# Turning each tile's rows one step later in a mixture-of-experts feed-forward: before this tile's gate and up products instead of after the tile's two places ahead

## The chip, the cores and the metric

The kernel runs on one core of one Trainium2 chip. The metric is the device time of one execution in microseconds (us); smaller is better. The kernel before takes 4045.59 us, the median of 3 runs (4045.33 to 4053.72).

## The reference, cut to what matters

The input is 8192 rows of 512 numbers. A modulated linear layer gives `xf`; a feed-forward follows that adds a shared expert and 8 of 64 routed experts for each row; the input is added at the end. Routing biases make the experts' sizes very unequal.

```python
# y: modulated 512x512 layer with a clip; xf = y.reshape(8192, 512)
shared = silu(xf @ sh_gate_w) * (xf @ sh_up_w) @ sh_down_w            # hidden 1024
topk_idx, w = _route(xf, router_w, e_bias)                            # 8 of 64 experts
order = argsort(topk_idx.reshape(-1), stable=True); tok = order // K
g = ragged_dot(xf[tok], gate_w, group_sizes)                          # 512 -> 256
u = ragged_dot(xf[tok], up_w, group_sizes)
o = ragged_dot(silu(g) * u, down_w, group_sizes)                      # 256 -> 512
routed = zeros_like(xf).at[tok].add(o * w.reshape(-1)[order][:, None])
return x + (shared + routed)
```

## The kernel before

The program has a dense phase (the modulated layer, the shared expert, the routing; some 1430 us) and a routed phase, which the change touches. In the routed phase the rows of each expert stand in tiles of 128 rows: 532 tiles, handled in one loop in groups of four (`UN = 4`; tile j has place `u = j % 4`). Each engine has its own in-order program, written by hand, and they meet at semaphores.

What happens to a tile j:
- SyncE loads two index lists; GpSimd gathers the 128 rows of `y_rows` into `x_rows` by an indirect DMA (L1036).
- TensorE turns the rows in four 128x128 transposes (`turn_x`, L1090). ScalarE copies them from PSUM as the high part `x_h` in fp32r (`x_high`, L1161), VectorE takes the rest, `x_l` (`x_low`, L30).
- TensorE does gate and up together: 4 slices of the contraction, for each the products high*high, high*low, low*high, 12 matmuls of 512 columns (`gate_up`, L1099). It waits for `x_l` of the tile and for `split`, which counts the parts of the expert's weights that VectorE has finished.
- ScalarE `silu` (L1167) and VectorE `hidden` (L1258) make `e_hf`; TensorE turns it (`turn_h`, 2 transposes in fp32, L1108); ScalarE and VectorE part it in `e_h_h` (L1173) and `e_h_l` (L30).
- TensorE `down` (L1117): 6 matmuls of 512 columns; ScalarE `weigh` (L1181) scales the result to `o_rows`; GpSimd adds it to the output by an indirect DMA (L1052).

One step of TensorE works on three tiles: gate and up of j, the turned rows of j+2, `turn_h` of j-1, `down` of j-2. A new expert's weights (three DMAs of 512 KB issued by SyncE, L998 and L1000) are cast on ScalarE (L1186) and parted on VectorE (L30, `w_gu_l`, `w_dn_l`); this happens in 29 places, two steps ahead of the expert's first tile: part 0 (`w_gu`, 1536 columns) in one step, parts 1 and 2 (512 and 1024 columns) at the beginning of VectorE's next step.

Of the kernel before, what the change touches and what calls it, by code (L numbers as in the profile page):

```python
# [32 lines left out]
def build(nc, x, cond, cw, cbias, aff_w, aff_b, router_w, e_bias, gate_w, up_w, down_w,  # L33
# [18 lines left out]
    UN = 4  # L52
# [17 lines left out]
    with top:  # L70
# [46 lines left out]
        with ExitStack() as tmp:  # L117
# [29 lines left out]
            @blk.sync  # L147
            def _(sp):
                sp.dma_start(aw_raw[:], aff_w.rearrange("(k p) w -> p k w", p=P)).then_inc(ld_aff, 16)
                sp.dma_start(cond_raw[:], cond).then_inc(ld_aff, 16)  # L150
                sp.dma_start(w_raw[:], cw.rearrange("(k p) c -> p k c", p=P)).then_inc(ld_w, 16)
                sp.dma_start(rw_raw[:], router_w).then_inc(ld_r, 16)
                with nc.allow_non_contiguous_dma(reason="small columns"):
                    sp.dma_start(ab[:], aff_b.rearrange("(k p) -> p k", p=P)).then_inc(ld_small, 16)
                    sp.dma_start(bias_c[:], cbias.rearrange("(k p) -> p k", p=P)).then_inc(ld_small, 16)
                sp.dma_start(eb[:], e_bias.partition_broadcast(P)).then_inc(ld_small, 16)
                for n, w in enumerate((sh_gate, sh_up, sh_down)):
                    if n == 1:
                        sp.dma_start(xin[:], xf[0:TB, :].rearrange("(t p) c -> p t c", p=P)).then_inc(x_ld, 16)
                    sp.dma_start(stage[n][:], w.rearrange("(k p) h -> p k h", p=P)).then_inc(ld_sh[n], 16)  # L160
# [740 lines left out]
        with ExitStack() as tmp:  # L901
# [42 lines left out]
            def field(eng, j, f, top_val):  # L944

                return eng.value_load(trow[0:1, bass.ds(j * FLD + f, 1)], min_val=0 if f != 5 else 4, max_val=top_val)  # L946
# [134 lines left out]
            @blk.tensor  # L1081
            def _(pe):
                pe.wait_ge(tab_ld, 16)
                pe.sem_inc(pe_do, 1)

                def turn_x(j, u, g):

                    pe.wait_ge(x_ld[u], 16 * (g + 1))
                    for k in range(KC):
                        last = nc.tensor.transpose(b_x[u % 2][:, k * P:(k + 1) * P].bitcast(F32R),  # L1090
                                                   xg[u][:, k * P:(k + 1) * P].bitcast(F32R), ident_r[:])
                    last.then_inc(pe_x, 1)

                def gate_up(j, u, place):

                    pe.wait_ge(dve_x, j + 1)
                    for k in range(KC):
                        for a, b in ((0, 0), (0, 1), (1, 0)):
                            last = nc.tensor.matmul(b_gu[u % 2][:], xp[a][:, u % 2, k, :],  # L1099
                                                    wgu[b][:, bass.ds(place, 1), k, :].rearrange("p a n -> p (a n)"),  # L1100
                                                    start=(k == 0 and a == b == 0), stop=(k == KC - 1 and a == 1))
                    last.then_inc(pe_gu, 1)

                def turn_h(j, u):

                    pe.wait_ge(dve_gu, j + 1)
                    for k in range(KH):
                        last = nc.tensor.transpose(b_h[u % 2][:, k * P:(k + 1) * P], hf[:, u % 2, k * P:(k + 1) * P], ident[:])  # L1108
                    last.then_inc(pe_ht, 1)

                def down(j, u, place):
                    if not isinstance(j, int) or j >= 2:
                        pe.wait_ge(act_do, j - 1)
                    pe.wait_ge(dve_ht, j + 1)
                    for k in range(KH):
                        for a, b in ((0, 0), (0, 1), (1, 0)):
                            last = nc.tensor.matmul(b_o[u % 2][:], hp[a][:, u % 2, k, :],  # L1117
                                                    wdn[b][:, bass.ds(place, 1), k, :].rearrange("p a n -> p (a n)"),
                                                    start=(k == 0 and a == b == 0), stop=(k == KH - 1 and a == 1))
                    last.then_inc(pe_do, 1)  # L1120

                def step(g, u, turn):

                    j = g * UN + u
                    place = turn.place(u)
                    pe.wait_ge(split, 3 * turn.order(u) + 3 + SPLIT_0)
                    gate_up(j, u, place)
                    turn_x(j + 2, (u + 2) % UN, g + 1 if u >= UN - 2 else g)
                    if not isinstance(j, int) or j >= 1:
                        turn_h(j - 1, (u - 1) % UN)  # L1130
                    if not isinstance(j, int) or j >= 2:
                        down(j - 2, (u - 2) % UN, turn.place(u - 2))

                pe.wait_ge(ident_ok, 1)
                pe.wait_ge(words, 1)
                turn_x(0, 0, 0)
                turn_x(1, 1, 0)
                for g in range(2):
                    turn = Turn(pe, g)
                    for u in range(UN):  # L1140
                        step(g, u, turn)
                last_turn = field(pe, 0, 5, NTURN - 1)
                with pe.Fori(2, NTURN) as g:
                    with pe.If(last_turn >= g):
                        turn = Turn(pe, g)
                        for u in range(UN):
                            step(g, u, turn)
                end = UN * last_turn + UN - 1
                turn_h(end, UN - 1)
                down(UN * last_turn + UN - 2, UN - 2, field(pe, UN * last_turn + UN - 2, 1, E) & (RING - 1))  # L1150
                down(end, UN - 1, field(pe, end, 1, E) & (RING - 1))

            @blk.scalar
            def _(act):
                act.wait_ge(tab_ld, 16)

                def x_high(j, u):
                    act.wait_ge(pe_x, j + 1)
                    if not isinstance(j, int) or j >= 2:
                        act.wait_ge(pe_gu, j - 1)  # L1160
                    nc.scalar.copy(xp[0][:, u % 2, :, :].rearrange("p k t -> p (k t)"), b_x[u % 2][:]).then_inc(act_x, 1)  # L1161
# [13 lines left out]
                def weigh(j, u, g):  # L1175

                    act.wait_ge(pe_do, j + 2)
                    act.wait_ge(ls_ld[u], 16 * (g + 1))
                    if not isinstance(j, int) or j >= UN:
                        act.wait_ge(added[u], 16 * g)  # L1180
                    nc.scalar.activation(og[u][:], b_o[u % 2][:], ACT.Copy, scale=ls[u][:, 1:2].bitcast(F32)).then_inc(act_do, 1)  # L1181
# [21 lines left out]
                def step(g, u, turn):  # L1203
                    j = g * UN + u
                    known = isinstance(j, int)
                    if not known or j >= 3:
                        weigh(j - 3, (u - 3) % UN, g - 1 if u < 3 else g)
                    with act.If(turn.first(u + 2) > 0):
                        start_weights(j + 2, turn.order(u + 2))
                    silu(j, u)  # L1210
                    x_high(j + 2, (u + 2) % UN)
                    if not known or j >= 1:
                        h_high(j - 1, (u - 1) % UN)
                    with act.If(turn.first(u + 2) > 0):
                        end_weights(turn.order(u + 2))
# [2 lines left out]
                start_weights(None, 0)  # L1218
                end_weights(0)
                x_high(0, 0)  # L1220
                x_high(1, 1)
                turn = Turn(act, 0)
                with act.If(turn.first(1) > 0):
                    start_weights(None, turn.order(1))
# [19 lines left out]
            def _(dve):  # L1244
# [4 lines left out]
                def x_low(j, u):  # L1249
                    dve.wait_ge(act_x, j + 1)  # L1250
                    sub_exact(nc, xp[1][:, u % 2, :, :].rearrange("p k t -> p (k t)"), b_x[u % 2][:],
                              xp[0][:, u % 2, :, :].rearrange("p k t -> p (k t)")).then_inc(dve_x, 1)
# [22 lines left out]

                def step(g, u, turn):
                    j = g * UN + u
                    with dve.If(turn.first(u + 1) > 0):
                        weights_low(turn.order(u + 1), (1, 2))
                    hidden(j, u)  # L1280
                    x_low(j + 2, (u + 2) % UN)
                    if not isinstance(j, int) or j >= 1:
                        h_low(j - 1, (u - 1) % UN)
                    with dve.If(turn.first(u + 2) > 0):
                        weights_low(turn.order(u + 2), (0,))
# [23 lines left out]
                dve.wait_ge(words, 1)  # L1309
                weights_low(0, (0, 1, 2))  # L1310
                x_low(0, 0)
                x_low(1, 1)
                turn = Turn(dve, 0)
                with dve.If(turn.first(1) > 0):
                    weights_low(turn.order(1), (0,))
# [40 lines left out]
```

## Time and profile before

| | us |
|---|---|
| median of 3 runs | 4045.59 |
| the profiled execution's own time | 4045.33 |
| its span, first to last instruction | 4043.6 |
| PE busy | 3891.3 (96%) |
| PEld busy | 3190.3 (79%) |
| POOL, DVE, ACT busy | 1916.6, 1649.8, 1444.2 |

PE is TensorE's matmuls, PEld its loads of the stationary operand, which can run beside a matmul. A matmul's shown duration contains its way through the array, so neighbouring ones overlap in the rows; what one costs is the distance from its start to the next start. DVE is VectorE, ACT ScalarE, POOL GpSimd, SP SyncE. Two consecutive instructions of one kind stand in one row of the timeline, with their count.

### The profile page before, as it was taken

How to read it: one execution, taken by the hardware profiler on the slowest of the kernel's cores; microseconds unless marked ns; L12 is line 12 of the kernel's file. 1: busy time of each engine (PE TensorE's matmuls, PEld its weight loads, DVE VectorE, ACT ScalarE, POOL GpSimd, SP SyncE). 2: the span in 40 equal slices, each digit the busy share in tenths (PEclk: the TensorE clock that was granted, in tenths of full speed). 3: DMA queues.
4: the chain of work that ended last, by engine and by line, in shares of the span. 5: the costliest groups of instructions: out<-in, count | busy, mean ns of one | idle time of the engine just before them, and what ended most of it. 6: DMA issues, size and time to landing. Idle time of an engine off the chain costs nothing.

```text
span 4043.6 us, 90661 instructions
## 1 busy us (share of the span) xinstructions
PE 3891.3 (96%) x19158; PEld 3190.3 (79%) x19159; DVE 1649.8 (41%) x3503; ACT 1444.2 (36%) x2807; POOL 1916.6 (47%) x1598
## 2 busy tenths in 40 slices
PE   7999999999999879999999999998899999999997
PEld 6888788888888658888888877886688888888886
DVE  4555555555555433333332333334433333333332
ACT  3222222222222123433433444445434343444333
POOL 1333333333333535555555555554455555555554
PEclk9999999999999889999999999999999999999998
DMA  5112211122111056666766666777776666676665
GB/s 175 42 48 58 64 43 43 48 58 63 42 42 50 24 107 114 124 116 112 138 115 114 126 133 125 125 128 194 168 119 123 116 125 114 126 127 125 114 113 104
DMA packets 372970, 408.94 MB, mean 101 GB/s; under 512 B 192457, under 2 KB 227409, under 8 KB 372881
## 3 DMA queue, kind: packets, MB, share of 16 engines
q0 software_dynamic: 135872, 280.60, 38.6%
q1 hardware_dynamic: 237010, 127.35, 12.4%
q8 instruction: 34, 0.56, 0.1%
q14 instruction: 54, 0.44, 0.1%
HBM read 228.83 MB, written 178.93 MB: 101 GB/s over the span
## 4 chain that ended last, share of the span: by engine, by line
PE 41%; DMA 9%; SPq 6%; issue 6%; DVE 0%; ACT 0%; POOLq 0%; DVEq 0%; ACTq 0%; POOL 0%
PE bank L1099 24%; PE bank L1117 12%; DMA out_dram<-o_rows,list_s 6%; SPq L946 4%; PE bank L1090 3%; PE bank L1108 2%; DMA list_g<-slot_list 2%; SPq L981 2%; DMA raw_d<-in_L_ffn_down_w_dram 1%; DMA raw_gu<-in_L_ffn_up_w_dram 1%; SPq L998 0%; DVE w_dn_l L30 0%; POOLq L946 0%; DMA list_s<-slot_list 0%; SPq L1000 0%
## 5 line engine op out<-in xcount | busy, mean ns | idle before, releaser
L1052 POOL DMA_INDIRECT out_dram<-o_rows,list_s x532 | 862.0, 1620 | 668.4 <-issue 352.5
L1258 DVE TENSOR_TENSOR e_hf<-bank,e_sg 128x256 f32<-128x256 f32 x532 | 225.8, 424 | 1669.0 <-ACT e_sg L1167 965.5
L406 POOL DMA_INDIRECT slot_list<-ent,pos x512 | 498.6, 974 | 860.6 <-PE bank L430 708.1
L1099 PE MATMUL bank<-w_gu_h,x_h 128*128 x2128 | 842.2, 396 | 33.9 <-DVE w_dn_l L30 31.3
L1099 PE MATMUL bank<-w_gu_h,x_l 128*128 x2128 | 837.5, 394 | 0.0
L1099 PE MATMUL bank<-w_gu_l,x_h 128*128 x2128 | 832.9, 391 | 0.0
L1036 POOL DMA_INDIRECT x_rows<-y_rows,list_g x536 | 536.9, 1002 | 563.0 <-issue 345.9
L1167 ACT ACTIVATE e_sg<-bank 128x256 f32<-128x256 f32 x532 | 204.6, 385 | 985.5 <-PE bank L1099 687.3
L1181 ACT ACTIVATE o_rows<-bank,list_s 128x512 f32<-128x512 f32 x532 | 367.0, 690 | 444.8 <-PE bank L1117 390.4
L1099 PEld LDWEIGHTS bank<-w_gu_h,x_h 128*128 128x128 f32 x2128 | 402.1, 189 | 130.8 <-issue 47.6
L1117 PE MATMUL bank<-w_dn_h,e_h_h 128*128 x1064 | 472.1, 444 | 4.8 <-DVE e_h_l L30 2.5
L1099 PEld LDWEIGHTS bank<-w_gu_h,x_l 128*128 128x128 f32 x2128 | 402.3, 189 | 91.1
L1099 PEld LDWEIGHTS bank<-w_gu_l,x_h 128*128 128x128 f32 x2128 | 402.4, 189 | 87.4
L1117 PE MATMUL bank<-w_dn_h,e_h_l 128*128 x1064 | 422.4, 397 | 0.0
L1117 PE MATMUL bank<-w_dn_l,e_h_h 128*128 x1064 | 419.8, 395 | 0.0
L30 DVE TENSOR_TENSOR x_l<-bank,x_h 128x512 fp32r<-128x512 f32 x534 | 369.1, 691 | 31.0 <-ACT x_h L1161 3.1
L1090 PEld LDWEIGHTS bank<-ident_r,x_rows 128*128 128x128 f32 x2136 | 240.0, 140 | 109.2 <-issue 25.7
L1161 ACT CAST x_h<-bank 128x512 fp32r<-128x512 f32 x534 | 313.5, 587 | 6.0 <-PE bank L1090 5.8
L1090 PE MATMUL bank<-ident_r,x_rows 128*128 128x128 f32 x2136 | 246.4, 239 | 35.8 <-DMA x_rows<-y_rows,list_g 35.6
L1117 PEld LDWEIGHTS bank<-w_dn_h,e_h_l 128*128 128x128 f32 x1064 | 200.8, 189 | 52.5
L616 ACT CAST h_h<-stage_d 128x512 fp32r<-128x512 f32 x128 | 79.4, 620 | 425.1 <-DVE stage_d L688 362.9
L1117 PEld LDWEIGHTS bank<-w_dn_h,e_h_h 128*128 128x128 f32 x1064 | 201.5, 189 | 33.9 <-issue 7.4
(203 smaller groups left out, 5711.2 us busy)
## 6 DMA issues: line engine op xcount, KB each, us to landing
xin<-in_x_dram SPq DMA_DIRECT2D x16, 1024.0 KB
y_rows<-yrow SPq DMA_DIRECT2D x64, 256.0 KB
stage_d<-in_x_dram SPq DMA_DIRECT2D x16, 1024.0 KB
out_dram<-stage_d SPq DMA_DIRECT2D x16, 1024.0 KB
raw_gu<-in_L_ffn_gate_w_dram SPq DMA_DIRECT2D x29, 512.0 KB
raw_gu<-in_L_ffn_up_w_dram SPq DMA_DIRECT2D x29, 512.0 KB
raw_d<-in_L_ffn_down_w_dram SPq DMA_DIRECT2D x29, 512.0 KB
list_g<-slot_list SPq DMA_DIRECT2D x536, 1.0 KB
```

Of the source, the lines that this page charges most:

```text
L30: return nc.vector.tensor_tensor(out, full, high.bitcast(F32), ALU.subtract)
L406: nc.gpsimd.indirect_dma_start(slots, bass.IndirectOffsetOnAxis(ap=pos[v][:, t, k:k + 1], axis=0), ent[v][:, t, k, :], None).then_inc(scat ...
L946: return eng.value_load(trow[0:1, bass.ds(j * FLD + f, 1)], min_val=0 if f != 5 else 4, max_val=top_val)
L1036: nc.gpsimd.indirect_dma_start(xg[u][:], None, y_rows, bass.IndirectOffsetOnAxis(ap=lg[u][:, 0:1].bitcast(U32), axis=0)).then_inc(x_ld[u], 16)
L1052: nc.gpsimd.indirect_dma_start(out, bass.IndirectOffsetOnAxis(ap=ls[u][:, 0:1].bitcast(U32), axis=0), og[u][:], None, compute_op=ALU.add). ...
L1090: last = nc.tensor.transpose(b_x[u % 2][:, k * P:(k + 1) * P].bitcast(F32R), xg[u][:, k * P:(k + 1) * P].bitcast(F32R), ident_r[:])
L1099: last = nc.tensor.matmul(b_gu[u % 2][:], xp[a][:, u % 2, k, :], wgu[b][:, bass.ds(place, 1), k, :].rearrange("p a n -> p (a n)"), start=( ...
L1117: last = nc.tensor.matmul(b_o[u % 2][:], hp[a][:, u % 2, k, :], wdn[b][:, bass.ds(place, 1), k, :].rearrange("p a n -> p (a n)"), start=(k ...
L1161: nc.scalar.copy(xp[0][:, u % 2, :, :].rearrange("p k t -> p (k t)"), b_x[u % 2][:]).then_inc(act_x, 1)
L1167: nc.scalar.activation(sg[:, u % 2, :], b_gu[u % 2][:, 0:H], ACT.Silu).then_inc(act_gu, 1)
L1181: nc.scalar.activation(og[u][:], b_o[u % 2][:], ACT.Copy, scale=ls[u][:, 1:2].bitcast(F32)).then_inc(act_do, 1)
L1258: nc.vector.tensor_tensor(hf[:, u % 2, :], b_gu[u % 2][:, H:2 * H], sg[:, u % 2, :], ALU.mult).then_inc(dve_gu, 1)
```

## The change

`turn_x`, `x_high` and `x_low` work one tile ahead, at the beginning of a step, and no longer two tiles ahead in its middle. TensorE's step becomes: turn j+1, gate and up of j, `turn_h` of j-1, `down` of j-2. On ScalarE `x_high` stands ahead of `weigh` and of the weights' first cast; it stood behind `silu`. On VectorE `x_low` stands ahead of the weights' parts 1 and 2; it stood behind `hidden`. The second tile's turn ahead of the loop goes.

```diff
@@ TensorE
 def step(g, u, turn):
     j = g * UN + u
+    turn_x(j + 1, (u + 1) % UN, g + 1 if u == UN - 1 else g)
     place = turn.place(u)
     pe.wait_ge(split, 3 * turn.order(u) + 3 + SPLIT_0)
     gate_up(j, u, place)
-    turn_x(j + 2, (u + 2) % UN, g + 1 if u >= UN - 2 else g)
     if not isinstance(j, int) or j >= 1:
         turn_h(j - 1, (u - 1) % UN)
...
 turn_x(0, 0, 0)
-turn_x(1, 1, 0)
@@ ScalarE
+    x_high(j + 1, (u + 1) % UN)
     if not known or j >= 3:
         weigh(j - 3, (u - 3) % UN, g - 1 if u < 3 else g)
     with act.If(turn.first(u + 2) > 0):
         start_weights(j + 2, turn.order(u + 2))
     silu(j, u)
-    x_high(j + 2, (u + 2) % UN)
...
 x_high(0, 0)
-x_high(1, 1)
@@ VectorE
+    x_low(j + 1, (u + 1) % UN)
     with dve.If(turn.first(u + 1) > 0):
         weights_low(turn.order(u + 1), (1, 2))
     hidden(j, u)
-    x_low(j + 2, (u + 2) % UN)
...
 x_low(0, 0)
-x_low(1, 1)
```

TensorE in a step of the loop, before: the last of the 12 gate and up matmuls, then both kinds of transposes in a row.

```order
L1099 MATMUL bank<-w_gu_h,x_l 128x512
L1088 ISA
L1090 MATMUL bank<-ident_r,x_rows 128x128 [waits x_rows_ld2]
L1090 MATMUL bank<-ident_r,x_rows 128x128 x3
L1108 MATMUL bank<-ident,e_hf 128x128 [waits dve_gu]
L1108 MATMUL bank<-ident,e_hf 128x128
```

The same place now:

```order
L1099 MATMUL bank<-w_gu_h,x_l 128x512
L1108 MATMUL bank<-ident,e_hf 128x128 [waits dve_gu]
L1108 MATMUL bank<-ident,e_hf 128x128
L1113 REGISTER_ALU
L1114 REGISTER_ALU [waits act_do]
```

And the passage from `down` to the next gate and up, now:

```order
L1117 MATMUL bank<-w_dn_h,e_h_l 128x512
L1090 MATMUL bank<-ident_r,x_rows 128x128 [waits x_rows_ld2]
L1090 MATMUL bank<-ident_r,x_rows 128x128 x3
L1127 REGISTER_ALU x2
L1127 ISA
L1096 REGISTER_ALU [waits split]
L1099 REGISTER_ALU [waits dve_x]
L1099 ISA
L1099 MATMUL bank<-w_gu_h,x_h 128x512
```

The six short matmuls between two long ones have become four ahead of gate and up, and two ahead of `down`.

VectorE where a new expert's weights are parted, before (`x_l` stands after the weights and `e_hf`):

```order
L30 TENSOR_TENSOR w_gu_l<-raw_gu,w_gu_h 128x1536
L1284 UNCONDITIONAL_BRANCH
L1278 COMPARE_AND_BRANCH
L1268 ISA
L30 REGISTER_ALU [waits w_high]
L30 ISA
L30 REGISTER_ALU
L30 ISA
L30 TENSOR_TENSOR w_gu_l<-raw_gu,w_gu_h 128x512
```

The same place now:

```order
L30 TENSOR_TENSOR w_gu_l<-raw_gu,w_gu_h 128x1536
L1282 UNCONDITIONAL_BRANCH
L30 TENSOR_TENSOR x_l<-bank,x_h 128x512 [waits act_x]
L1277 COMPARE_AND_BRANCH
L1266 ISA
L30 REGISTER_ALU [waits w_high]
L30 ISA
L30 REGISTER_ALU
L30 ISA
L30 TENSOR_TENSOR w_gu_l<-raw_gu,w_gu_h 128x512
```

`x_l`, with its wait for ScalarE's `act_x`, now stands between the first part of the weights and the other two.

## Rows read from the trace of the kernel before

**Rows 1.** The page: the chain that ended last, shares of the span

```profile
PE 41%; DMA 9%; SPq 6%; issue 6%; DVE 0%; ACT 0%; POOLq 0%; DVEq 0%; ACTq 0%; POOL 0%
```

**Rows 2.** Timeline of one step, matmuls: start us, us, engine, line, operation, count

```profile
3000.20 0.40 PE L1099 MATMUL bank<-w_gu_h,x_h 128*128 x1
...
3002.94 0.46 PE L1090 MATMUL bank<-ident_r,x_rows 128*128 128x128 f32 x4
3003.23 0.41 PE L1108 MATMUL bank<-ident,e_hf 128*128 128x128 f32 x2
...
3004.88 0.40 PE L1099 MATMUL bank<-w_gu_h,x_h 128*128 x1
...
3009.57 0.40 PE L1099 MATMUL bank<-w_gu_h,x_h 128*128 x1
```

**Rows 3.** Timeline of the same step, loads from the fp32 transposes on

```profile
3003.20 0.20 PEld L1108 LDWEIGHTS bank<-ident,e_hf 128*128 128x128 f32 x2
...
3003.26 0.14 PEld L1108 LDWEIGHTS bank<-ident,e_hf 128*128 128x128 f32 x1
3003.37 0.19 PEld L1117 LDWEIGHTS bank<-w_dn_h,e_h_h 128*128 128x128 f32 x1
3003.48 0.19 PEld L1117 LDWEIGHTS bank<-w_dn_l,e_h_h 128*128 128x128 f32 x1
3003.72 0.19 PEld L1117 LDWEIGHTS bank<-w_dn_h,e_h_l 128*128 128x128 f32 x1
```

**Rows 4.** Timeline of the dense phase, loads after 64-column bf16 matmuls

```profile
97.45 0.19 PEld L497 LDWEIGHTS bank<-mask,ones 128*128 128x128 bf16 x4
97.57 0.19 PEld L430 LDWEIGHTS bank<-sh_down_h,h_h 128*128 128x128 f32 x1
97.68 0.19 PEld L430 LDWEIGHTS bank<-sh_down_l,h_h 128*128 128x128 f32 x1
```

**Rows 5.** Timeline of the dense phase, loads after eight transposes

```profile
137.88 0.19 PEld L430 LDWEIGHTS bank<-cols_l,sh_gate_h 128*128 128x128 f32 x1
...
140.42 0.19 PEld L430 LDWEIGHTS bank<-cols_h,sh_up_h 128*128 128x128 f32 x1
...
141.10 0.19 PEld L430 LDWEIGHTS bank<-cols_h,sh_up_h 128*128 128x128 f32 x1
```

**Rows 6.** Timeline of the step of rows 2, VectorE and ScalarE

```profile
3004.05 0.69 DVE L30 TENSOR_TENSOR x_l<-bank,x_h 128x512 fp32r<-128x512 f32 x1
3005.08 0.69 ACT L1181 ACTIVATE o_rows<-bank,list_s 128x512 f32<-128x512 f32 x1 [0.79 <-issue]
```

**Rows 7.** Waits, routed phase: engine, line, what for, us in total, times, longest

```profile
PE bank L1099 <- DVE w_dn_l L30: 31.3, 24, 2.1
...
PEld bank L1090 <- DMA x_rows<-y_rows,list_g: 13.5, 10, 3.3
...
SPq L946 <- DMA out_dram<-o_rows,list_s: 280.2, 207, 7.4
```

**Rows 8.** Timeline at a new expert's weights, ScalarE, VectorE and PE

```profile
3691.45 1.48 ACT L1186 CAST w_gu_h<-raw_gu  x1 [1.92 <-DMA raw_gu<-in_L_ffn_up_w_dram]
...
3694.33 0.41 DVE L30 TENSOR_TENSOR e_h_l<-bank,e_h_h 128x256 fp32r<-128x256 f32 x1
...
3694.36 1.06 ACT L1186 CAST w_dn_h<-raw_d  x1
...
3694.96 1.76 DVE L30 TENSOR_TENSOR w_gu_l<-raw_gu,w_gu_h  x1 [0.22 <-issue]
3697.03 0.69 DVE L30 TENSOR_TENSOR w_gu_l<-raw_gu,w_gu_h  x1 [0.30 <-issue]
3697.63 1.22 DVE L30 TENSOR_TENSOR w_dn_l<-raw_d,w_dn_h  x1
...
3699.19 0.51 PE L1099 MATMUL bank<-w_gu_h,x_h 128*128 x1 [1.14 <-DVE w_dn_l L30]
```

**Rows 9.** Waits from 2764 to 2920 us, where small experts follow each other

```profile
PEld bank L1090 <- DMA x_rows<-y_rows,list_g: 13.1, 9, 3.3
```

## The prediction

> **What bounds the kernel now.** I read the page's chain first: TensorE has 41% of it and no other engine's work shows at all [rows 1]; the waits and DMAs that share it are ones that TensorE mostly does not stand still for. Then the timeline of one step far from a weight change. Gate and up of one tile start at 3000.20, of the next at 3004.88, of the next at 3009.57: a step takes 4.69 us, with TensorE never idle [rows 2]. 532 steps of 4.69 are 2495 us of the routed phase, so what happens inside TensorE's own stream is the term to get right. Last the waits: TensorE stands still for the weights' last part (31.3 us in 24 places) and for gathered rows (13.5 us, 10 places) [rows 7]. All other engines have slack in a plain step.
>
> **TensorE's step, by starts.** Nothing is added or taken from a step: 18 long matmuls (512 columns), 4 transposes of `x_rows`, 2 of `e_hf`. Only neighbours change, so I price the borders. [...] Behind a long matmul (0.23 from start to start) every load is hidden. Behind a short one it may not be. The rows give the borders:
> - The loads of `e_hf` begin at 3003.20 and 3003.26 [rows 3]: 0.06 apart. So behind the last `x_rows` transpose, the first `e_hf` load costs no more than 0.06.
> - The next load begins at 3003.37 (0.11 for the fp32 transpose), the one after at 3003.48: again 0.11, either the second transpose or the load of `e_h_h` [rows 3].
> - Which of the two it is tells the dense phase: behind bf16 matmuls that follow each other by 0.03 (four loads in 0.19), the fp32r operand's load begins at 97.57 and the next at 97.68 [rows 4]. With nothing long ahead of it an fp32r load costs 0.11 by itself.
>
> Before, the six short ones stand together: four `x_rows`, two `e_hf`, then `down`. After, `x_h`'s first load stands behind the last `x_rows` transpose: 0.11 instead of the 0.06 of `e_hf`. The first `e_hf` load is now behind a long matmul and hidden; its transpose (0.11) and `down`'s first load (0.11) are as before. The border of `down` to gate and up (0.23) becomes `down` to `x_rows` (0.23), that of gate and up to `x_rows` becomes gate and up to `e_hf` (0.23). Net: 0.11 - 0.06 = 0.05 us a step; times 532, **27 us slower**.
>
> [...]
>
> **A second, smaller term.** Long matmuls are a little slower for a while after short ones. In the dense phase, the 11 loads from 137.88 to 140.42 follow eight transposes and take 2.54, 0.231 each; the next three take 0.68, 0.227 each [rows 5]. So one burst costs 0.04 over the next ten or so. The routed step pays this once now: the 12 from 3000.20 to 3002.94 take 2.74, only 0.02 over 12 times 0.227 [rows 2], since they are the tail's end; the rest of the tail lies in `down`. With two bursts, gate and up pay their own tail, 0.04 instead of 0.02. `down` pays as before, or less because only two short ones stand ahead of it. From both sides: +0.03 a step if both tails are whole, -0.04 if they shrink with the burst; the dense rows are the nearest for gate and up, so I take +0.015, **8 us** in 532 steps.
>
> **What the late turn costs the other engines.** Counted from the first `x_rows` transpose (3002.94) to the end of `x_l` (3004.05 + 0.69) it takes 1.8 us [rows 2, 6]. Now the turn of j+1 starts about 0.3 ahead of gate and up of j, and the result is wanted a step later, after 4.7. Some 2.9 us of slack stay: no cost in a plain step. If something held `x_high` for longer than that, TensorE would wait for the difference. `weigh` has to stand behind `x_high`: `o_rows` begins 0.2 after the first gate and up matmul now [rows 2, 6]; it will begin about 0.7 after it. Its PSUM bank is not wanted for more than a step, so the 0.5 costs nothing there, but the scatter, and behind it SyncE, which waits for scatters 207 times [rows 7], start 0.5 us later relative to TensorE. Behind SyncE's wait stand the index lists and the weights' DMAs. The lists feed gathers whose turn is 1.9 us later than before, so they gain; the weights lose up to 0.5 us.
>
> **At a new expert.** The chain runs from the cast of `w_gu_h` at 3691.45, once the DMA has landed, to gate and up at 3699.19: 7.7 us [rows 8]. VectorE does in it `e_hf`, `x_l`, `e_h_l` and then the three parts of the weights. After, the same work stands in another order: `e_hf`, `e_h_l`, part 0 (0.7 us earlier), `x_l`, parts 1 and 2. The new head of the queue, `x_l`, waits for ScalarE's `x_high`, which stands behind the two last weight casts, and for TensorE to have turned j+2 after `down`. ScalarE's last cast ends 4.0 after 3691.45 now (3694.36 + 1.06); with `x_high` (about 0.6, an estimate from `x_l`'s 0.69 on the same elements) taken from ahead of it that is 3.4 or 3.5, and `x_high` ends at 4.1. Part 0 ends 5.3 after now (3694.96 + 1.76), 4.6 then [rows 8]. So `x_l` just fits and the 7.7 stays. I cost the 24 waits at 0.1 us each for their later landing (0.5 later, less what five longer steps of lead, 0.07 each, give back): **3 us**. From both sides: -0.7 each if VectorE's earlier start shortened the chain, +0.7 each if `x_l` waits, so -17 to +17.
>
> **Gathered rows.** 13.5 us in 10 places [rows 7], of which 13.1 in 9 places lie where small experts follow each other [rows 9] and the weights end the wait anyway. I count nothing; at most 10 us go. One turn, one `x_high`, one `x_low` go at the end: -0.4.
>
> **Sum.** 27 + 8 + 3 - 0.4 = 38 us against the profiled execution's own 4045.33 (span 4043.6, 1.7 around it), which is the median of the runs to 0.3: **4083 us**, 0.9% slower.
>
> **The rivals.**
> - [...] Chance 0.08.
> - *A faster kernel.* The place is VectorE's queue at a new expert. If part 0, 0.7 us earlier, brings the last part 0.7 earlier in 24 waits, that is 17 us; with the gather waits gone, another 10. That is 27 us, and together with a border that costs nothing and a tail that does not grow, 4045 - 27 = 4018. It wins once the border costs under 0.05 us a step. For it: `x_l` stands later now, and rows wait longer to be turned. Against it: parts 1 and 2 still stand behind `x_l`. Chance 0.04.
> - *A new wait on x.* `x_high` or TensorE's order makes `x_l` late at each new expert, and gate and up of plain steps wait at times. If the 29 changes of weights cost 0.7 each, that is 20 us on top of 35: 4101. For it: the fit above is half a microsecond. Chance 0.13.
> - Forecast, the borders and tails: chance 0.75.
>
> **Range and chances.** The likeliest case alone reaches from 27 - 9 to 27 + 17 + 5, that is 4063 to 4094, and the new wait to 4101. I give 4062 to 4097. What a measurement of this kernel tells from no change is 0.2%, 8 us. Slower by more: 0.75 + 0.13, and a third of the first rival: 0.91. Faster by more: 0.04. Within: 0.05.
>
> **What would show it.** In the profile after, a plain step from one gate and up to the next takes 4.75 (right: 4.73 to 4.77; 4.69 says that the border is hidden). The second load of gate and up begins 0.11 after the first, and 0.23 between the two `e_hf` loads. The waits for `w_dn_l` stay near 31 us; over 50 says that `x_l` is in the way. Waits for gathered rows go down. I am wrong if the step is the same, or if the time comes from another wait than TensorE's stream.

## The result, and the profile after

| | before | after |
|---|---|---|
| median of 4 runs | 4049.65 us (4045.33 to 4055.8) | 4081.88 us (4079.21 to 4090.57) |
| ratio | | 1.0082, 95% interval 1.0059 to 1.0105 |
| span of the profiled execution | 4043.6 us | 4088.2 us |

The kernel is slower by 0.8%. The forecast was 4083 us. That the time itself came out within 1 us of it is in part luck: the forecast was 38 us more than 4045.33, the medians measured here are 32.2 us apart (24 to 43 by the interval), and the kernel before was 4 us slower in this comparison. The profiled execution after is one of the slower ones: its span is 44.6 us longer, of which 7.3 lie ahead of the routed phase, in the dense phase that the change does not touch. The granted clock of TensorE was 0.78 there in the first 101 us, and 0.97 in the profile before; at 111 us the profile after is already 4.3 us behind. The first turn of rows starts at 1442.58 before and at 1449.88 after. These two rows are of before and then of after, matmuls by start:

```profile
1442.58 0.72 PE L1090 MATMUL bank<-ident_r,x_rows 128*128 128x128 f32 x4 [24.92 <-DMA x_rows<-y_rows,list_g]
```

```profile
1449.88 0.72 PE L1090 MATMUL bank<-ident_r,x_rows 128*128 128x128 f32 x4 [24.53 <-DMA x_rows<-y_rows,list_g]
```

From the first gate and up to the last it is 2563.5 us before and 2602.1 after, 38.6 more. That is the change's.

A plain step after, matmuls (start, duration, both in us), answers to [rows 2]:

```profile
3002.46 0.46 PE L1090 MATMUL bank<-ident_r,x_rows 128*128 128x128 f32 x4
3002.76 0.46 PE L1099 MATMUL bank<-w_gu_h,x_h 128*128 x1
...
3005.60 0.38 PE L1108 MATMUL bank<-ident,e_hf 128*128 128x128 f32 x2
...
3007.22 0.46 PE L1090 MATMUL bank<-ident_r,x_rows 128*128 128x128 f32 x4
3007.51 0.46 PE L1099 MATMUL bank<-w_gu_h,x_h 128*128 x1
```

From one turn of rows to the next it is 4.76 us, 0.07 more than the 4.69 before. Over all plain steps the median is 4.687 before and 4.760 after, and it hardly varies. 531 intervals of 0.073 are 38.8 us: the whole difference of the routed phase.

The loads of the same step (PEld), which answer to [rows 3], show where the 0.07 is:

```profile
3002.72 0.19 PEld L1099 LDWEIGHTS bank<-w_gu_h,x_h 128*128 128x128 f32 x1
3002.83 0.19 PEld L1099 LDWEIGHTS bank<-w_gu_l,x_h 128*128 128x128 f32 x1
3003.06 0.19 PEld L1099 LDWEIGHTS bank<-w_gu_h,x_l 128*128 128x128 f32 x1
...
3005.37 0.37 PEld L1108 LDWEIGHTS bank<-ident,e_hf 128*128 128x128 f32 x2
...
3005.60 0.14 PEld L1108 LDWEIGHTS bank<-ident,e_hf 128*128 128x128 f32 x1
3005.71 0.19 PEld L1117 LDWEIGHTS bank<-w_dn_h,e_h_h 128*128 128x128 f32 x1
3005.82 0.19 PEld L1117 LDWEIGHTS bank<-w_dn_l,e_h_h 128*128 128x128 f32 x1
```

From the load of `x_h` behind the last turned row to the next load it is 0.11 (3002.72 to 3002.83), where it was 0.06 from the load of `e_hf`. The first `e_hf` load now lies under a long matmul: 0.23 to the second. From there it is 0.11 and 0.11 to the next two, as before. The 11 loads from 3002.83 to 3005.37 take 2.54, just what the 11 loads behind eight transposes of the dense phase took [rows 5].

TensorE's waits of the routed phase after answer to [rows 7]:

```profile
PE bank L1099 <- DVE w_dn_l L30: 40.0, 27, 3.2
PE bank L1090 <- DMA x_rows<-y_rows,list_g: 25.8, 2, 24.5
PE bank L1108 <- DVE e_hf L1256: 13.0, 6, 5.6
```

The second row is now only the start of the phase (24.5 us, which the window of rows 7 left out). Waits for gathered rows in the loop are gone. Waits for the weights went from 31.3 to 40.0 us, and 13.0 us for `e_hf` are there. The 531 intervals from one gate and up to the next, less 531 plain steps, hold 74.7 us before and 74.5 after: outside plain steps nothing was gained or lost, as far as one profile each can tell.

Waits are not all that these 75 us hold. TensorE's waits of the loop, all rows of the answer without the one at the end of the phase, are 50.1 us before and 55.5 after. Some of the rest is the granted clock. In these rows of the kernel before, the clock is at the upper of its two levels at first (granted clock 1.00) and at the lower one (0.50 from 2797.7 to 2801.1) soon after a wait:

```profile
2796.28 0.49 PE L1099 MATMUL bank<-w_gu_h,x_h 128*128 x1 [2.10 <-DVE w_dn_l L30]
2796.61 0.39 PE L1099 MATMUL bank<-w_gu_l,x_h 128*128 x1
2796.84 0.39 PE L1099 MATMUL bank<-w_gu_h,x_l 128*128 x1
...
2798.24 0.63 PE L1099 MATMUL bank<-w_gu_l,x_h 128*128 x1
2798.66 0.63 PE L1099 MATMUL bank<-w_gu_h,x_l 128*128 x1
```

A long matmul then takes 0.43 us from start to start instead of 0.23. Every such fall within the loop, in this trace and in that of the kernel after, comes behind a wait of 1.4 us or more. At the lower level the loop spends 34 us before, some 30 of them with TensorE at work, and 27 us after. By 0.43 against 0.23 that costs some 14 us before and 11 after, an estimate. The forecast had no term for it.

### The profile page after: what moved, and what is told of

The parts are those of the page before. It is cut to its first block, busy times and chain, and to the rows that moved or that the text cites. A ratio compares the mean times of both kernels' runs of the same rounds, so it can differ in the third digit from the quotient of the medians.

```text
span 4088.2 us, 90388 instructions
## 1 busy us (share of the span) xinstructions
PE 3924.2 (96%) x19154; PEld 3196.6 (78%) x19155; DVE 1649.8 (40%) x3502; ACT 1435.3 (35%) x2806; POOL 1937.9 (47%) x1598
## 4 chain that ended last, share of the span: by engine, by line
PE 48%; DMA 7%; SPq 4%; issue 4%; DVE 0%; POOLq 0%; DVEq 0%; ACT 0%; POOL 0%; ACTq 0%
PE bank L1099 29%; PE bank L1117 14%; DMA out_dram<-o_rows,list_s 4%; PE bank L1090 3%; SPq L946 2%; PE bank L1108 2%; DMA raw_d<-in_L_ffn_down_w_dram 1%; DMA list_g<-slot_list 1%; SPq L981 1%; SPq L998 0%; DVE w_dn_l L30 0%; POOLq L946 0%; DMA raw_gu<-in_L_ffn_up_w_dram 0%; SPq L1000 0%; POOL x_rows L1036 0%
## 5 line engine op out<-in xcount | busy, mean ns | idle before, releaser
L1052 POOL DMA_INDIRECT out_dram<-o_rows,list_s x532 | 871.9, 1639 | 804.4 <-DMA list_g<-slot_list 455.3
L1099 PE MATMUL bank<-w_gu_h,x_h 128*128 x2128 | 883.4, 415 | 40.3 <-DVE w_dn_l L30 40.0
L1036 POOL DMA_INDIRECT x_rows<-y_rows,list_g x536 | 545.9, 1018 | 446.7 <-issue 277.6
L30 DVE TENSOR_TENSOR e_h_l<-bank,e_h_h 128x256 fp32r<-128x256 f32 x532 | 220.8, 415 | 7.1 <-ACT e_h_h L1172 7.1
```

The lines of the kernel that those rows point to most:

```text
L30: return nc.vector.tensor_tensor(out, full, high.bitcast(F32), ALU.subtract)
L1036: nc.gpsimd.indirect_dma_start(xg[u][:], None, y_rows, bass.IndirectOffsetOnAxis(ap=lg[u][:, 0:1].bitcast(U32), axis=0)).then_inc(x_ld[u], 16)
L1052: nc.gpsimd.indirect_dma_start(out, bass.IndirectOffsetOnAxis(ap=ls[u][:, 0:1].bitcast(U32), axis=0), og[u][:], None, compute_op=ALU.add). ...
```

## The experiments

Each was timed beside the kernel before on the same chip. That kernel's median differs from chip to chip (4020.94 us beside the first four, 4046.62 beside the next four, 4041.58 beside the last), so only ratios to it are compared. Waits and clocks are of one profile of each kernel.

### TensorE's order alone

```diff
-                    gate_up(j, u, place)
-                    turn_x(j + 2, (u + 2) % UN, g + 1 if u >= UN - 2 else g)
+                    pe.wait_ge(dve_x, j + 1)
+                    turn_x(j + 2, (u + 2) % UN, g + 1 if u >= UN - 2 else g)
+                    gate_up(j, u, place)
```

> The kernel before, still turning rows two tiles ahead, with ScalarE's and VectorE's programs untouched; on TensorE alone the turn of j+2 is put ahead of gate and up of j (behind the wait for x_l of j, which frees its PSUM bank). Theory A (the price is in TensorE's stream: a load behind the last short transpose costs 0.11 instead of 0.06 us, and a second burst makes the following long matmuls a little slower): a plain step takes 4.76 us as in the kernel after, the whole about 38 us more than before, ratio 1.008 to 1.010. Rival B (the price is the later turn of the rows, or the new places of x_high and x_low on ScalarE and VectorE): a plain step stays at 4.69, ratio 1.000.

Measured: ratio 1.009 (1.0075 to 1.0104). From turn to turn:

```profile
3000.97 0.46 PE L1090 MATMUL bank<-ident_r,x_rows 128*128 128x128 f32 x4
...
3005.73 0.46 PE L1090 MATMUL bank<-ident_r,x_rows 128*128 128x128 f32 x4
```

4.76 us, and the same loss as the whole change, with the rows turned two tiles ahead and the other engines' programs untouched. The price is TensorE's order. Rival B, that it is the later turn or the new places on ScalarE and VectorE, falls.

The order also moved the waits. These rows answer to [rows 7]:

```profile
PE bank L1090 <- DMA x_rows<-y_rows,list_g: 40.1, 20, 3.6
...
PE bank L1090 <- DVE w_dn_l L30: 4.0, 6, 2.0
```

The turn now stands first in TensorE's step, so TensorE waits there for late rows (40.1 us, 9.2 before) and hardly for the weights any more (4.0, 31.3 before).

### The change with one burst

```diff
                     turn_x(j + 1, (u + 1) % UN, g + 1 if u == UN - 1 else g)
+                    if not isinstance(j, int) or j >= 1:
+                        turn_h(j - 1, (u - 1) % UN)
                     place = turn.place(u)
...
                     gate_up(j, u, place)
-                    if not isinstance(j, int) or j >= 1:
-                        turn_h(j - 1, (u - 1) % UN)
```

> The kernel after, with the two transposes of e_hf put right behind the four of x_rows, ahead of gate and up: six short matmuls in one burst again, the rows still turned only one tile ahead. Theory A: the borders are those of before (0.06 for the first e_hf load, 0.11 for the fp32r load behind an fp32 transpose), a plain step 4.69, the whole within 10 us of before, ratio 0.998 to 1.002. Rival B (the later turn costs): 4.76 and 1.009 stay.

Measured: ratio 1.0023 (1.0014 to 1.0032). A plain step, and TensorE's largest wait:

```profile
3000.13 0.46 PE L1090 MATMUL bank<-ident_r,x_rows 128*128 128x128 f32 x4
3000.42 0.41 PE L1108 MATMUL bank<-ident,e_hf 128*128 128x128 f32 x2
3000.59 0.49 PE L1099 MATMUL bank<-w_gu_h,x_h 128*128 x1
...
3004.82 0.46 PE L1090 MATMUL bank<-ident_r,x_rows 128*128 128x128 f32 x4
```

```profile
PE bank L1108 <- DVE e_hf L1256: 44.2, 20, 8.6
```

The plain step is back at 4.69, so the loss goes with the burst and not with the later turn: this is theory A's main sentence. The whole, 11.5 us by the medians, is just outside what I gave. The `e_hf` transposes now stand ahead of gate and up, and at new experts TensorE waits 44.2 us for them in 20 places. But these waits took the place of others: all of TensorE's waits in the loop are 48.6 us, 50.1 in the kernel before. Over plain steps the intervals hold 85 us all the same, where those of the kernel before hold 75 and those of the first experiment's kernel 63. What did grow is the time at the lower clock level, 51 us of the loop instead of 34 (granted clock 0.94 from 2600 to 3000, and 0.96 before): by the prices above some 6 of the 10 us, an estimate. No run changes the clock by itself, so this is read from the traces and not shown.

### The two e_hf transposes first

```diff
-                    turn_x(j + 2, (u + 2) % UN, g + 1 if u >= UN - 2 else g)
                     if not isinstance(j, int) or j >= 1:
                         turn_h(j - 1, (u - 1) % UN)
+                    turn_x(j + 2, (u + 2) % UN, g + 1 if u >= UN - 2 else g)
```

> The kernel before, with the two e_hf transposes ahead of the four of x_rows: one burst of six as before, in the other order. Theory A by the loads: after the hidden first load 0.11, 0.11, 0.08, 0.08, 0.09 and then 0.11 for down's fp32r load behind a short transpose, 0.59 instead of 0.54: a plain step 4.73 to 4.75, about 27 us more than before, ratio 1.0065. Rival C (each separate burst of short matmuls costs 0.07, whatever is loaded): still one burst, so 4.69 and ratio 1.000.

Measured: ratio 1.0033 (1.0023 to 1.0043). Two neighbouring steps' `e_hf` transposes, and loads of the first:

```profile
3002.91 0.38 PE L1108 MATMUL bank<-ident,e_hf 128*128 128x128 f32 x2
...
3007.64 0.38 PE L1108 MATMUL bank<-ident,e_hf 128*128 128x128 f32 x2
```

```profile
3002.91 0.14 PEld L1108 LDWEIGHTS bank<-ident,e_hf 128*128 128x128 f32 x1
3003.02 0.42 PEld L1090 LDWEIGHTS bank<-ident_r,x_rows 128*128 128x128 f32 x4
...
3003.38 0.19 PEld L1117 LDWEIGHTS bank<-w_dn_h,e_h_h 128*128 128x128 f32 x1
3003.49 0.19 PEld L1117 LDWEIGHTS bank<-w_dn_l,e_h_h 128*128 128x128 f32 x1
```

One burst, the same six instructions, and yet 4.73 us: the order within the burst costs, so rival C (so much for each burst) falls. The borders are as expected: 0.11 from load to load twice in a row from the second `e_hf` load on, and 0.11 from `down`'s first load, which stands behind a short matmul, to its second; from the second load of the burst to `down`'s second it is 0.58 (3002.91 to 3003.49), where it was 0.54. The whole is half of what I gave, and the step is under it too: half of the plain steps take 4.71 and half 4.73, 4.717 in the mean, where I gave 4.73 to 4.75: the borders bring 0.043, and the long matmuls were 0.013 quicker. Theory A has no account of that.

### Three transposes singly

```diff
-                def gate_up(j, u, place):
+                def gate_up(j, u, place, g):
...
+                    v = (u + 2) % UN
                     for k in range(KC):
                         for a, b in ((0, 0), (0, 1), (1, 0)):
...
-                    last.then_inc(pe_gu, 1)
+                        if k == KC - 1:
+                            last.then_inc(pe_gu, 1)
+                        if k == 0:
+                            pe.wait_ge(x_ld[v], 16 * ((g + 1 if u >= UN - 2 else g) + 1))
+                        turned = nc.tensor.transpose(b_x[v % 2][:, k * P:(k + 1) * P].bitcast(F32R),
+                                                     xg[v][:, k * P:(k + 1) * P].bitcast(F32R), ident_r[:])
+                    turned.then_inc(pe_x, 1)
...
-                    gate_up(j, u, place)
-                    turn_x(j + 2, (u + 2) % UN, g + 1 if u >= UN - 2 else g)
+                    gate_up(j, u, place, g)
```

> The kernel before, with the four x_rows transposes of j+2 one by one behind the four slices of gate and up (the fourth still stands ahead of the e_hf pair): four places with short matmuls instead of one. Theory A: three singles cost a border of 0.11 each, the burst of three 0.06 + 0.11 + 0.11, together 0.61 instead of 0.54, and all long matmuls run at the tail's 0.231 instead of 0.227 or 0.229, another 0.03 to 0.05: a step of 4.79 to 4.81, 53 to 65 us more than before, ratio 1.013 to 1.016. Rival C (0.07 for each further burst): three more bursts, 0.21 a step, 112 us more, ratio 1.028.

Measured: ratio 1.0104 (1.0088 to 1.0119).

```profile
3001.30 0.39 PE L1100 MATMUL bank<-w_gu_h,x_h 128*128 x1
...
3006.09 0.39 PE L1100 MATMUL bank<-w_gu_h,x_h 128*128 x1
...
3010.87 0.39 PE L1100 MATMUL bank<-w_gu_h,x_h 128*128 x1
```

Steps of 4.79 and 4.78 alternate from gate and up to gate and up, 4.784 in the mean: 52 us in 532 steps, at the lower end of what theory A gave for the step. The whole, 42 us more, is under its ratio of 1.013 to 1.016: a miss in size. Rival C's 112 us are far off. The difference lies in the intervals outside plain steps and was not followed.

### Weigh ahead of x_high

```diff
-                    x_high(j + 1, (u + 1) % UN)
                     if not known or j >= 3:
                         weigh(j - 3, (u - 3) % UN, g - 1 if u < 3 else g)
+                    x_high(j + 1, (u + 1) % UN)
```

> The kernel after, with ScalarE's weigh ahead of x_high again (x_high stays one tile ahead). It tests the prediction's term for the later scatter and the weights' later landing. Theory A: TensorE's plain step stays 4.76; o_rows starts 0.2 us after gate and up instead of 0.7 or more; the waits at new experts change by a tenth of a microsecond each, 3 us in all, so the ratio to before is 1.007 to 1.010. Rival B (x_high ahead of weigh costs on ScalarE): the ratio falls to 1.004 or less.

Measured: ratio 1.006 (1.004 to 1.0081), between the two expectations, and its interval overlaps that of the kernel after. The step stays 4.76. TensorE's waits:

```profile
PE bank L1099 <- DVE w_dn_l L30: 42.7, 18, 3.6
PE bank L1108 <- DVE e_hf L1256: 4.7, 1, 4.7
```

Against the kernel after, the waits for `e_hf` are 8 us less and those for the weights 3 us more. Whether that comes from this order or from the execution is not settled by one profile each.

### Weights issued one tile earlier

```diff
-                    if not known or n >= 2:
-                        weights(n - 1)
+                    if not known or n >= 1:
+                        weights(n)
```

> The kernel before, with SyncE issuing a new expert's weights one tile earlier (in the step of the tile itself, not one after). It tests what the 76 us outside plain steps hang on. Theory L (they hang on the landing of the weights, so on when SyncE issues them): outside the run of small experts the 12 or so waits of 0.8 to 1.6 us vanish, within it the DMA stays the bound: 10 to 20 us less than before, ratio 0.995 to 0.998, plain step 4.69. Rival V (they hang on VectorE's queue of 7.7 us from the first cast on): ratio 0.999 to 1.001.

Measured: ratio 0.999 (0.9979 to 1.0001), no difference that counts.

```profile
PE bank L1090 <- DMA x_rows<-y_rows,list_g: 35.6, 13, 8.4
PE bank L1099 <- DVE w_dn_l L30: 15.2, 15, 2.1
```

The number is rival V's and the mechanism is theory L's: the wait for the weights halves, 31.3 to 15.2 us, and a wait for gathered rows takes its place, 9.2 to 35.6 us. One engine issues both. Together TensorE's waits of the loop are 53.0 us, 50.1 before.

### One burst, weights one tile earlier

The edits of the second experiment and of the one above together.

> The one-burst kernel (rows turned one tile ahead, the e_hf transposes right behind them) with the weights issued one tile earlier. In the one-burst kernel TensorE stands 44 us at e_hf, because ScalarE, waiting for the weights, holds silu back. Theory L: about half of that goes, ratio to before 0.996 to 1.000, plain step 4.69. Rival V: 1.002 stays.

Measured: ratio 1.0005 (0.9993 to 1.0018), between the two expectations. Its interval overlaps that of the one-burst kernel, so whether the earlier weights brought anything is not clear. Theory L's half of the waits did not go:

```profile
PE bank L1108 <- DVE e_hf L1256: 41.9, 17, 6.1
```

44.2 has become 41.9 us. Most of these waits (32.9 us, from 2700 to 2960) lie among the small experts.

### Weights issued two tiles earlier, or behind the second list

```diff
-                    if not known or n >= 2:
-                        weights(n - 1)
+                    if not known or n >= 1:
+                        if known and n == 1:
+                            weights(1)
+                        weights(n + 1)
```

> The kernel before, with the weights issued two tiles earlier. Theory L: hardly more than one tile earlier brings, since one tile is 4.7 us and the landing is late by 1 to 3 us: ratio 0.994 to 0.998. If among the small experts the earlier wait for a free half of the buffer holds back the index lists, gathers come late and it is worse than one tile earlier, 0.998 to 1.001.

Measured: ratio 1.0086 (1.0066 to 1.0106), worse than either expectation. TensorE's and SyncE's waits:

```profile
PE bank L1092 <- DMA x_rows<-y_rows,list_g: 61.5, 14, 8.6
```

```profile
SPq L990 <- DVE w_dn_l L30: 67.9, 8, 10.8
```

SyncE waits 67.9 us for a free half of the weights' buffer (L990 here), and all index lists stand behind it. TensorE's waits of the loop are 76.9 us together, 27 more than before, but the intervals over plain steps hold 40 more (115 us). The clock goes with the long waits: the granted clock from 2760 to 2960 is 0.78, where it was 0.93, and the loop spends 92 us at the lower level, 63 of them with TensorE at work. By the prices above that is some 15 us more than before, an estimate.

The last one issues `weights(n)` behind `load_list` of the second list, at the end of SyncE's step:

```diff
-                    if not known or n >= 2:
-                        weights(n - 1)
...
                         load_list(ls[(u - LAG_S) % UN], ls_ld[(u - LAG_S) % UN], m)
+                    if not known or n >= 1:
+                        weights(n)
```

> The kernel before, with the weights issued in the step of the tile itself, but behind that step's second index list instead of ahead of it. With the weights one tile earlier ahead of that list, TensorE's waits for w_dn_l halved (31 to 15 us) and its waits for gathered rows rose (from 9 to 36). Theory S (SyncE's wait for a free half and for the last weights' landing holds the lists back): the second list goes first, scatters and the gathers behind them come earlier, the waits for rows go down to 10 to 25 us: ratio 0.995 to 0.998. Rival G (it is the next step's first list, list_g, that is held, and it stands behind the weights as before): the waits for rows stay over 30 us, ratio 0.998 to 1.001.

Measured: ratio 1.0081 (1.0065 to 1.0096).

```profile
PE bank L1090 <- DMA x_rows<-y_rows,list_g: 63.4, 25, 6.2
...
PE bank L1099 <- DVE w_dn_l L30: 2.2, 2, 1.9
```

The weights are hardly waited for any more, and rows 63.4 us. Rival G had the waits for rows (over 30 us), and both expectations missed the size. Why it costs more than with the weights ahead of that list stays open. No version beat the kernel before.

## Why the prediction was right

**TensorE's borders: right, and shown.** The step of the argument was 0.11 instead of 0.06 behind the last turned row, 27 us. In the profile after, the medians over all steps are 108 ns at that load and 232 at the hidden `e_hf` load, against 230 and 59 before: 51 ns net, 27 us. TensorE's order alone gives the loss back in full, one burst takes it away, and the order within a burst changes it without a second burst.

That every load behind a long matmul is hidden shows in rows like these of the kernel before, a long matmul, the load that runs beside it and that load's own matmul:

```profile
3000.43 0.39 PE L1099 MATMUL bank<-w_gu_l,x_h 128*128 x1
3000.43 0.19 PEld L1099 LDWEIGHTS bank<-w_gu_h,x_l 128*128 128x128 f32 x1
3000.66 0.40 PE L1099 MATMUL bank<-w_gu_h,x_l 128*128 x1
```

The load is through at 3000.62, 0.04 ahead of its matmul. Over the routed phase, before and after, the load behind a long matmul starts with it (within 0.004 in the median, for each kind of load) and ends 0.04 ahead of its own matmul, or 0.09 where the load is that of a transpose (0.14 long). The matmuls' shown durations are longer than their distances by much the same time: a long one 0.39 for 0.23, a turned row 0.23 for 0.07. Behind a short matmul a load and its own matmul lie otherwise. These are a load of [rows 3], the matmul that belongs to it, and the next load:

```profile
3003.37 0.19 PEld L1117 LDWEIGHTS bank<-w_dn_h,e_h_h 128*128 128x128 f32 x1
3003.39 0.49 PE L1117 MATMUL bank<-w_dn_h,e_h_h 128*128 x1
3003.48 0.19 PEld L1117 LDWEIGHTS bank<-w_dn_l,e_h_h 128*128 128x128 f32 x1
```

The matmul is shown from 0.02 after its own load's start, 0.17 ahead of that load's shown end (3003.56), and the next load begins 0.09 after the matmul. So the border's price from load to load is measured, 0.11 here. Whether the load or the matmul ahead of it makes it is not shown; that an fp32r load takes 0.11 by itself was my estimate from [rows 4].

**The tail: right in kind, a little small.** I took 0.015 a step, 8 us. The long matmuls of gate and up took 0.024 more together, those of `down` 0.008 less; the four turned rows themselves 0.005 more, which I had not counted. That is 0.021, 11 us. The picture was a little off as well: the one tail before holds 0.06 over ten matmuls (by the medians of the distances, against 0.227), not 0.04, and the two tails after hold 0.04 and 0.03. In the experiment with the `e_hf` transposes first the long matmuls took 0.013 less in a way that I can't work out. What makes it is open.

**The other engines in a plain step: right.** These rows of the kernel after are of ScalarE and VectorE in the step shown above:

```profile
3003.59 0.69 ACT L1180 ACTIVATE o_rows<-bank,list_s 128x512 f32<-128x512 f32 x1
3003.72 0.69 DVE L30 TENSOR_TENSOR x_l<-bank,x_h 128x512 fp32r<-128x512 f32 x1 [1.51 <-ACT x_h L1160]
```

`x_l` is through at 3004.41, 1.95 after the turn (I had 1.8) and 3.1 before the gate and up that reads it (3007.51). `o_rows` starts 0.83 after gate and up (I had 0.7). Neither holds up a plain step.

**New experts and gathered rows: the sum right in part by luck, its parts not.** I gave +3 us for the weights and nothing for the rows. Outside plain steps it is 74.7 us before and 74.5 after. In that, waits rose by 5 us, and some 3 us came back, by the estimates above (14 and 11), because less time was spent at the lower clock level (34 us before, 27 after), which I had not priced. The waits for the weights rose by 9 us and not 3 (40.0 is neither near the 31 nor over the 50 that I named as signs), the waits of matmuls for rows in the loop, 9.2 us before, went, and TensorE waits 10 us longer for `e_hf`, which I had not named at all. The place of the longest such wait shows why. ScalarE in the kernel after:

```profile
2934.84 1.47 ACT L1185 CAST w_gu_h<-raw_gu  x1 [9.72 <-DMA raw_gu<-in_L_ffn_up_w_dram]
2936.22 0.38 ACT L1166 ACTIVATE e_sg<-bank 128x256 f32<-128x256 f32 x1
```

and TensorE behind it:

```profile
2937.11 0.69 PE L1108 MATMUL bank<-ident,e_hf 128*128 128x128 f32 x2 [5.59 <-DVE e_hf L1256]
```

`silu` stands behind a weight cast that waits 9.72 us for its DMA. Before, TensorE would have come later to these transposes, since it stood at the late rows first. By this reading one lack of weights shows up in the wait that comes first in TensorE's order. That the total nearly stayed fits this, the first experiment showed such an exchange by TensorE's order alone (weights 31.3 to 4.0, rows 9.2 to 40.1), and the early-weights experiment showed it by SyncE's. It was not shown separately for the change.

**The rivals.** The first, chance 0.08, that the loads are hidden anyway and nothing changes: refuted by the profile (a step of 4.76, not 4.69) and by the first experiment (4.76 as well). That VectorE's earlier part 0 makes it faster: its border term is refuted, and the waits for the weights rose. That `x_l` comes late at new experts: 20 us were its price, 9 appeared, set off by the rows; whether `x_l` is in them was not tried by itself.

## What to carry to other kernels

In a program whose TensorE never idles, the order of short and long matmuls can have a price of its own. Here it was 0.05 us a step in the borders (108 and 232 ns from load to load after, 230 and 59 before) and 0.02 in the tail. Read each border from the trace as the distance from load to load: here 0.23 behind a long matmul, and 0.11, 0.08 or 0.06 behind a short one. Try the short matmuls in one burst (4.69 a step here, 4.76 in two), and price the burst's order too (4.717 with the `e_hf` transposes first). Where one late transfer holds a chain, look for a wait that goes at the next wait in TensorE's order (31.3 to 4.0 for the weights and 9.2 to 40.1 for the rows in the first experiment), and sum them all before calling it a gain. Then look at the granted clock, for the sum of the waits was not the whole price: with nearly the same sum (48.6 and 50.1 us) the one-burst kernel's loop spent 51 us at the lower level and the kernel before 34, in one profile each.

## What the runs showed of the hardware that was not expected

- Behind short matmuls the distance from one load to the next was not the same for three kinds of 128x128 operand that the trace shows as f32: 0.06 us from the first load of the fp32 transposes (`e_hf`), 0.08 to 0.09 between those of the turned rows, read as fp32r, and 0.11 from that of an fp32r product (`x_h`, `e_h_h`). From the second `e_hf` load it was 0.11 too [rows 3]. Which part of a distance is the load's and which the matmul's is not shown.
- Long matmuls were slower for about ten behind short ones: 2.54 us for 11 loads instead of 2.50, with the same sum in two phases of the program.
- Weight DMAs issued earlier by SyncE, which also issues the index lists, were no gain. One tile earlier the waits for rows rose from 9.2 to 35.6 us and those for the weights fell from 31.3 to 15.2; two tiles earlier it was 61.5 us for rows, against 19 us less for the weights.
